# Second layer of a two-layer cross-attention kernel: which engine fetches the natural context, and in what place of the load order

## The reference, cut to what matters

```python
h = _layer_norm(x, ln1_scale, ln1_offset)
x = res + _cross_attention(h, xf_1, wq1, bq1, wk1, ...)   # 16 heads of 128
h = _layer_norm(x, ln2_scale, ln2_offset)
x = res + _cross_attention(h, xf_2, wq2, bq2, wk2, ...)
h = _layer_norm(x, ln_mlp_scale, ln_mlp_offset)
return x + gelu(h @ w_fc1 + b_fc1) @ w_fc2 + b_fc2
```

## Time and profile before

| | |
|---|---|
| median of three executions | 2400.6 us (2392.99 to 2402.63) |
| profiled execution, its own time | 2403.57 us |
| its span in the profile | 2401.7 us (1.9 us lie around it) |
| TensorE busy | 96% of the span |
| VectorE, ScalarE, GpSimd busy | 57%, 41%, 33% |
| mean granted TensorE clock | 0.986 |
| mean DMA traffic | 104 GB/s |

### The profile page before, as it was taken

How to read it: one execution, slowest core, us unless ns; L and a number is a source line. 1 busy time by engine, 2 the same in 40 slices (tenths; PEclk the granted TensorE clock), 3 DMA queues, 4 the chain that set the end, 5 groups by cost and what they waited for, 6 DMA issues and landing times. The chain is left out here.

```text
span 2401.7 us, 36559 instructions
## 1 busy us (share of the span) xinstructions
PE 2306.2 (96%) x13464; PEld 2076.4 (86%) x13464; DVE 1377.3 (57%) x3122; ACT 994.3 (41%) x2174; POOL 783.3 (33%) x839
## 2 busy tenths in 40 slices
PE   6898999999999999999999989999999999999999
PEld 6676899998989999998786769999999999999987
DVE  4797545454575455557539965454546655454572
ACT  3796434242433333343228944343334333242430
POOL 3142432415141414223641341514141423314054
PEclk8899999999999999999999999999999999999999
DMA  8631323233323323234453213333332334233322
GB/s 253 198 101 32 102 85 106 88 94 119 96 86 103 101 80 99 88 114 140 152 186 101 79 38 100 114 95 99 99 98 84 98 89 115 76 101 92 107 93 73
DMA packets 134580, 250.45 MB, mean 104 GB/s; under 512 B 31199, under 2 KB 54879, under 8 KB 133383
## 3 DMA queue, kind: packets, MB, share of 16 engines
q10 hardware_dynamic: 44600, 126.75, 17.3%
q1 hardware_dynamic: 89807, 121.38, 17.0%
HBM read 223.19 MB, written 29.48 MB: 105 GB/s over the span
## 5 line engine op out<-in xcount | busy, mean ns | idle before, releaser
L701 POOL TENSOR_SCALAR wk_hi<-raw 128x512 fp32r<-128x512 f32 (+1 forms) x92 | 59.2, 643 | 850.5 <-DMA raw<-in_wk 726.6
L1496 ACT ACTIVATE probs<-scores,prm 112x376 f32<-112x376 f32 x256 | 147.4, 576 | 334.6 <-DVE prm L1903 334.6
L837 PE MATMUL pj_two<-ctx_hi,wk_hi 128*128 128x376 f32 x688 | 235.3, 342 | 5.7 <-DVE rr L1658 3.9
L838 PE MATMUL pj_two<-ctx_lo,wk_hi 128*128 128x376 f32 x688 | 231.3, 336 | 0.0
L1658 DVE TENSOR_TENSOR rr<-pj_two,rr 128x448 fp32r<-128x448 f32 (+2 forms) x216 | 142.5, 661 | 154.5 <-ACT rr L1243 154.3
L839 PE MATMUL pj_two<-ctx_hi,wk_lo 128*128 128x376 f32 x688 | 230.6, 335 | 0.0
L703 POOL TENSOR_TENSOR wb_lo<-raw,wb_hi 128x512 fp32r<-128x512 f32 x152 | 197.9, 1302 | 12.7
L1660 DVE SCALAR_TENSOR_TENSOR k_lo<-pj_two,cur,k_hi 128x375 fp32r<-128x375 f32 x164 | 99.5, 607 | 168.5 <-ACT k_hi L1245 168.2
L1245 ACT ACTIVATE k_hi<-pj_two,cur 128x375 fp32r<-128x375 f32 x164 | 93.9, 573 | 243.9 <-PE pj_two L839 241.4
L837 PE MATMUL pj_two<-pt_hi,nat 125*128 125x448 f32 x510 | 190.6, 374 | 1.1
L839 PE MATMUL pj_two<-pt_hi,nat 125*128 125x448 f32 x510 | 187.7, 368 | 0.0
(11 more groups left out here) (350 smaller groups left out, 6685.5 us busy)
## 6 DMA issues: line engine op xcount, KB each, us to landing
nat<-nat_scratch ACTq DMA_DIRECT2D x256, 384.0 KB, 3.8
raw<-in_wq SPq DMA_DIRECT2D x72, 256.0 KB, 3.2
raw<-in_wo SPq DMA_DIRECT2D x72, 256.0 KB, 2.6
raw<-in_wk SPq DMA_DIRECT2D x64, 256.0 KB, 4.1
raw<-in_wv SPq DMA_DIRECT2D x64, 256.0 KB, 3.9
raw<-in_w SPq DMA_DIRECT2D x64, 256.0 KB, 2.9
nat_scratch<-rr ACTq DMA_DIRECT2D x7, 1536.0 KB, 6.6
k_hi<-keys_scratch SPq DMA_DIRECT2D x32, 188.0 KB, 2.7
```

Source lines behind the costliest of these rows:

```text
L701: nc.gpsimd.tensor_scalar(hi, src, 1.0, 0.0, ALU.mult, ALU.add).then_inc(split_hi, 1)
L837: nc.tensor.matmul(dst, l_hi, r_hi, start=first, stop=False)
L838: nc.tensor.matmul(dst, l_hi, r_lo, start=False, stop=False)
L1496: nc.scalar.activation(probs[0:L, h, 0:SK], scores[n % SCR][0:L, 0:SK], ACT.Exp, bias=neg_max[0:L, h:h + 1], accum_out=row_sum[0:L, h:h + ...
```

## The change

ScalarE issues no load of `nat` any more. SP issues all of them, with a wait of its own in front of each: for `r(b - 1, c)` finished on TensorE, or for b = 0 for the last read of the quarter in the group before (in a half's first group: for the first query product). `load_nat(0, c)` stands first in a group's part of SP's order, ahead of bx; `load_nat(b + 1, c)` stands behind `store_extra(b)`. Also, the next group's wk (or the first MLP weights) is moved from before `store_extra(3)` to behind it.

```diff
+                    def load_nat(b, c):
+                        sp.wait_ge(pj_ready, gpj + unit["r", b - 1, c] + 1 if b > 0 else nat_read[c])
+                        if b == 0 and c == 0:
+                            sp.sem_inc(sp_passed, 1)
+                        cols = slice(c * NQ, (c + 1) * NQ)
+                        sp.dma_start(nat[:, cols].bitcast(F32), nat_dram[hf * HB + b, :, cols]).then_inc(nat_in[c], 16)
...
+                    nat_read = [gpj + unit["q", 0] + 1 if ag == 0 else last_read[c] for c in range(DC)]
+                    for c in range(DC):
+                        load_nat(0, c)
                     if ag == 0:
                         sp.wait_ge(bx_out, 48)
...
-                    store_extra(0)
-                    store_extra(1)
-                    sp.wait_ge(pj_ready, gpj + unit["v", 0, HPG - 1] + 1)
-                    store_extra(2)
+                    for b in range(HB - 1):
+                        if b == HB - 2:
+                            sp.wait_ge(pj_ready, gpj + unit["v", 0, HPG - 1] + 1)
+                        store_extra(b)
+                        for c in range(DC):
+                            load_nat(b + 1, c)
+                    store_extra(HB - 1)
                     if ag + 1 < NG:
                         load_k(ag + 1)
+                        load_q(ag + 1)
                     else:
                         load_mlp(0)
-                    store_extra(3)
-                    if ag + 1 < NG:
-                        load_q(ag + 1)
+                    last_read = [gpj + unit["r", HB - 1, c] + 1 for c in range(DC)]
                     values_read = gpj + unit["v", 1, HPG - 1] + 1
...
-                def load_nat(b, c):
-                    cols = slice(c * NQ, (c + 1) * NQ)
-                    act.dma_start(nat[:, cols].bitcast(F32), nat_dram[hf * HB + b, :, cols]).then_inc(nat_in[c], 16)
...
                              pj_ready, gpj + unit + 1, mid=pj_mid)
-                        if b + 1 < HB:
-                            load_nat(b + 1, c)
...
                     exps1(0, 1)
-                    for c in range(DC):
-                        load_nat(0, c)
                     for b in range(1, HB):
```

## The result

| | before | after |
|---|---|---|
| median | 2395.0 us (7 runs, 2390.68 to 2402.63) | 2406.64 us (7 runs, 2404.78 to 2410.98) |
| profiled execution, its own time | 2403.57 us | 2405.19 us |
| its span | 2401.7 us | 2403.4 us |

The ratio is 1.0038, 95% interval [1.0023, 1.0054]: 9.1 us slower by the ratio, which is inside the half per cent (12 us) that the forecast called "same", but clear of zero. The first three executions of the kernel before had a median of 2400.6; with four more it is 2395.0, and in the later comparisons 2394.4 to 2398.3.

What follows compares the result with a forecast made beforehand. TensorE, busy 96% of the span, was taken to bound the kernel. Terms -3 + 4 + 1 = +2 us gave 2405.6 on the profiled execution, 2402.6 on the median; range 2391 to 2412.

Steps and rivals of the forecast that it cites:

- The start of a group: Without four ScalarE issues in a row, k(1, 0)'s move starts 0.9 us sooner, cutting the probabilities wait: 3 us won, bounds 5.6 and nothing.
- the lower bound's reason: At a group's start nothing might be won, since the normalisations also meet POOL's work and their phase shifts.
- Collisions at the four ends: At attention ends (g = 3) moved wk splits meet VectorE's layer norm: 1.0 us per end, 4 us lost, bounds nothing and 14.
- rival C: Layer norm stands behind POOL by the full lock rule: about 3 us at each of four ends, 2412.6 us; chance 0.08.
- The last query chunk at the second attention's start: At g = 0 nat's 1.5 MB runs beside the last wq chunk, already awaited: 0.5 us lost twice, 1 us in all.
- wk behind ex(3): Later wk and wq loads and splits cost 0: 5.4 us to spare before the first key product, 2.8 for wq's last chunk.
- rival B: Late query weights: wk behind store_extra(3) pushes wq 1 us too late in each of 14 groups, 2414.6 us; chance 0.10.
- nat's loads for b = 1 to 3: In SP's queue they wait for the same r(b - 1, c) as on ScalarE; a batch lasts some 19 us: cost 0.
- the first group of a half: SP loads nat, then wo and wv, until 1461; ex(0) follows, wanted at 1468.94: cost 0, hidden with 6 us.
- the MLP weights: Second half's context loads behind the first MLP chunks; the next set is split near 1138, wanted at 1144.51: cost 0, hidden.
- A: Rival: the group's start is worth all of its 5.6 us wait, with no loss elsewhere: 2395.0 us; chance 0.15.
- D: Rival: hidden anyway, ScalarE's free time hides the issues and the normalisations stay as they are: 2400.6 us; chance 0.12.

Runs made afterwards that it cites:

- f5: Kernel before, SP untouched; ScalarE issues nat's four first-sequence loads one at a time, each behind its move of a query product, instead of in a row: ratio 1.0003.
- f1: Kernel before with only the next group's wk (and the first MLP weights) moved behind ex(3), all nat loads left on ScalarE: ratio 1.0050, 2409.8 us.
- e1: Changed kernel, but only at the second attention's start nat's four first-sequence loads stand behind the wo chunks, not ahead of bx: 1.0019 of the kernel before.
- e3: Changed kernel with nat's first loads behind wo at the second attention's start and wk (and MLP weights) ahead of ex(3) again: 0.9980 of the kernel before.
- f3: As e3, but nat's first four loads stand behind wo in every group except a half's first: 0.9978 of the kernel before, 2391.3 us.
- e4: Kernel before, only nat's first-sequence loads (64 of 256) issued by SP, ahead of bx; the other 192 stay on ScalarE, wk ahead of ex(3): ratio 1.0000.
- g3: Kernel before with only the row bias of the first two sequences deferred behind the last pair's values at an attention's end: ratio 1.0020, 2398.5 us.
- g1: As f1, plus the row bias of the first two sequences deferred behind the last values at an attention's end: 1.0009 of the kernel before.
- e2: Changed kernel, but wk (and the MLP weights) issued ahead of nat's last-sequence loads and ex(3) again: 1.0010 of the kernel before, 2396.7 us.

## Why the prediction was right or wrong

The number held in its range (2406.6 in 2391 to 2412) and "same" was the right class, at +0.38%. But the median that it was built on was 5.6 us above that of seven runs, which hid part of the error: the change costs 9.1 us by the ratio and 10.0 by the stretches, where the sum said 2. So the number held by luck: one term of 1 us measured 10.5, two others came out near their size by other ways than those named, and the same range around the median of seven (2385.4 to 2406.4) would just have missed 2406.6. By its steps:

- *The start of a group, -3 us.* Right about the held-up move, wrong about what it frees. The move of k(1, 0) now starts 0.29 us after ScalarE's last work, released by TensorE (1.19 before, with the issues in front):

```profile
1658.63 0.57 ACT L1259 ACTIVATE k_hi<-pj,cur 128x375 fp32r<-128x375 f32 x1 [0.29 <-PE pj L853]
```
```profile
1664.35 1.25 DVE L1916 TENSOR_SCALAR probs<-probs,prm 112x376 f32<-112x376 f32 x1
```
```profile
1665.65 0.51 PE L856 MATMUL tp_two<-ident,probs 112*126 112x112 f32 x3 [0.47 <-DVE probs L1916]
```

But the wait for probabilities is 5.5 us, not 2: now the normalisation at 1664.35 meets a wv_lo pass of POOL (1663.98, 1.40 us) and takes 1.25, which was the lower bound's reason. Some gain is real: in the eight ordinary stretches the four kernels with ScalarE's four issues in a row have 880.6 to 881.0 us, the nine with SP issuing nat(0) 877.8 to 879.5. That is 2 us for eight groups, so the size of 3 was fair, but the mechanism named is not the one that the waits show: f5 frees the same move and has 7.8 us of this wait. Where the 2 us come from stays open.

- *Collisions at the four ends, +4 us, rival C 12.* The place, the engines and the row bias were named, and so was the wait (1.13 to about 2 us; it is 1.55 twice and 2.20 twice). The size depends on which of POOL's passes the row bias meets. In the changed kernel the stretches with an end grew by 4.0 us (-0.4, +2.8, +0.6, +1.0), just the forecast; the last two are long stretches that hold other drops of the clock as well. With wk moved alone (f1) the four grew by 13.3, about rival C's number. The 4 was right by luck, since it was built on an average: the earlier trace rows give 0.26 us for each of four instructions, but it was one instruction that was held up by most of a pass (0.68 to 1.75), directly in front of the one that TensorE awaits, and the wait then mostly cost as much again in clock, which the sum left out. The Trainium skill's rule (SBUF — State Buffer, Who interferes with whom), by which of two such instructions the one that comes second is blocked until the first is done, agrees with the row bias here: it began 0.72 us into a 1.91 us pass, ended 0.56 us behind it and took 1.07 us more than alone.

- *The last query chunk at the second attention's start, +1 us.* This is the step that failed: 0.5 us twice, with bounds of 0 and 2 each, and it was 5.1 and 5.4 us. That the chunk would land late was foreseen (it was 1.2 us), and that TensorE waits there already. Not foreseen were that a later split falls into the layer norm's instructions on VectorE, which gave another 1.3 us on POOL, and that behind a wait of 2.8 or 2.9 us the clock is at 0.50 for 6 us, another 3 us each time. e1 takes the whole term away.

- *wk behind ex(3), 0 in the ordinary groups.* Right, and rival B is out. In the changed kernel TensorE has no wait for POOL's wk_lo or wb_lo outside the two starts. POOL is done with wk at 1632.1, 5.1 us ahead of the next group's first key product at 1637.2 (5.4 forecast), and with wq at 1645.0, 7.8 us behind it (7.3 forecast, and 10.1 would be too late):

```profile
1622.58 0.62 POOL L715 TENSOR_SCALAR wk_hi<-raw 128x512 fp32r<-128x512 f32 x1 [64.85 <-DMA raw<-in_wk]
...
1630.82 1.29 POOL L717 TENSOR_TENSOR wk_lo<-raw,wk_hi 128x512 fp32r<-128x512 f32 x1
...
1643.71 1.29 POOL L717 TENSOR_TENSOR wb_lo<-raw,wb_hi 128x512 fp32r<-128x512 f32 x1
```

- *nat's loads for b = 1 to 3, the first group of a half, the MLP weights, 0 each.* Right. No wait for nat exists, a half's first groups are no longer than before (259.9 against 262.5), TensorE waits for no split of the MLP weights, and the loads land as well as before:

```profile
L626 SPq DMA_DIRECT2D nat<-nat_scratch x256: 319/326/1859, 243.9 to 2283.6; - x128
...
DMA to landing us min/median/max: 3.1/3.3/7.4
```

- *Rivals.* A (gain only, 2395.0) is about what e3 and f3 are against before, 4 us less, once the two losses are gone. D gives 2400.6, 6 us under the measured median. Its reason holds for ScalarE's issues (e4: 192 of them are worth nothing; f5: freeing the row of four is worth nothing either), but not for the normalisations, which do move, nor for the two losses.

Open: whether the later landing (1.2 us) would cause POOL's longer passes (1.3 us) every time, since e1 removes both, and f5 has one such pass without a late landing; what gives the 2 us in the ordinary groups, and why f5, which frees ScalarE's row as well, does not reach e3; what decides which pass the row bias meets; why the clock did not fall behind one wait of 2.20 us; and g3's loss.

## What to carry to other kernels

When a transfer or a split is moved, ask at each handover what it will lie beside, instruction by instruction, and take the worst meeting and not the mean where the instruction stands directly in front of one that the bounding engine awaits. Put a large load that has time to spare behind the small one that does not, even if it matters at only two places in the program. And compare stretches between two marks of the program, marks that the change itself does not move: two profiled spans 1.7 us apart held a loss of 10.

## What was not expected of the hardware

- In the groups of the second layer behind a half's first, over the fourteen profiled executions, TensorE's granted clock stayed at 1.00 behind every single wait of 0.5 to 1.9 us (1.13 before, 0.53 in g1, 1.86 in e2). Of the ten waits of 2.2 us it fell to 0.50 at nine, for 3.4 or 6.8 us, and not at the tenth (e1). At all three of 2.8 to 2.9 us it fell, for 6.8 us twice (after) and 3.4 once (e2). A matmul of 224 columns took 0.41 us there instead of 0.28. So at a start the clock's 3 us cost more than the 2.2 to 2.4 us by which the wait had grown.
- The collision goes both ways: VectorE's row bias went from 0.68 to 1.75 us and POOL's wk_lo pass beside it from 1.29 to 1.91; POOL's high part from 0.62 to 1.60.
- A 256 KB chunk with 1.5 MB issued right behind it landed in 4.1 us instead of 2.9.
